# Preparing the second batch and the output weights earlier in a fused attention and FFN layer

## The reference

```python
# B, S, H = 2, 1024, 1024; 32 heads of 32; F = 2752; all float32
x = x + attention(layernorm(x))        # qkv = xn @ Wqkv + bqkv; softmax(q k^T / sqrt(32)) v; ctx @ Wo + bo
xn = layernorm(x)                      # eps 1e-5, no scale or shift
x = x + (silu(xn @ Wg.T) * (xn @ Wu.T)) @ Wd.T
```

## Time and profile before

| | us |
|---|---|
| median of 3 runs | 3329.88 |
| lowest and highest run | 3327.52, 3333.98 |
| profiled execution, its own time | 3327.03 |
| its span in the profile | 3325.2 |
| PE busy | 3191.2 (96%) |
| DVE busy | 2013.0 (61%) |
| ACT busy | 1450.3 (44%) |
| POOL busy | 811.9 (24%) |

### The profile page before, as it was taken

The page is one execution under the profiler, slowest core; times in us unless marked ns, Lnnn a source line. Parts: engine busy times, 40 slices in busy tenths (PEclk is TensorE's granted clock), DMA queues, the critical chain, the costliest instruction groups (busy, mean ns, idle before and its releaser), DMA issues.

```text
span 3325.2 us, 38853 instructions
## 1 busy us (share of the span) xinstructions
PE 3191.2 (96%) x14464; PEld 2490.1 (75%) x14464; DVE 2013.0 (61%) x3093; ACT 1450.3 (44%) x2679; POOL 811.9 (24%) x604
## 2 busy tenths in 40 slices
PE   6999999988999999999799999999999999999999
PEld 5767777766777676776477888888888888888887
DVE  5789888887898888988774433232333423232324
ACT  1477787766777777778552111111111111111111
POOL 1224333332343343433433110101011010101010
PEclk9999999999999999999899999999999999999999
DMA  2434243342333433324556621111111411111111
GB/s 102 124 111 132 84 125 103 102 149 80 102 112 101 124 87 102 120 90 124 152 143 207 207 80 42 60 51 39 57 62 47 171 64 51 39 45 57 51 51 51
DMA packets 146028, 315.90 MB, mean 95 GB/s; under 512 B 24944, under 2 KB 58864, under 8 KB 142256
## 3 DMA queue, kind: packets, MB, share of 16 engines
q1 hardware_dynamic: 145840, 313.42, 30.3%
HBM read 228.41 MB, written 84.41 MB: 94 GB/s over the span
## 4 chain that ended last, share of the span: by engine, by line
PE 84%; DVE 13%; ACT 1%; DMA 1%; issue 1%; SPq 0%; POOL 0%; ACTq 0%; DVEq 0%
PE ps L659 16%; PE ps L660 15%; PE ps L661 15%; PE ps L725 6%; PE ps L744 6%; PE ps L756 5%; PE ps L761 5%; PE ps L814 5%; PE ps L815 5%; PE ps L816 5%; DVE mx L1046 4%; DVE pl L1068 4%; DVE wl L1018 2%; PE ps L686 1%; ACT ph L884 1%
## 5 line engine op out<-in xcount | busy, mean ns | idle before, releaser
L883 ACT ACTIVATE pu<-ps 128x512 f32<-128x512 f32 x1024 | 617.5, 603 | 412.0 <-PE ps L744 409.1
L1046 DVE TENSOR_REDUCE mx<-ps 128x1 f32<-128x512 f32 x1024 | 697.6, 685 | 157.1 <-PE ps L725 147.5
L1146 POOL TENSOR_TENSOR pl<-pu,ph 128x512 fp32r<-128x512 f32 x320 | 434.3, 1357 | 1011.6 <-ACT ph L884 1010.7
L884 ACT ACTIVATE ph<-ps 128x512 fp32r<-128x512 f32 x1024 | 616.4, 602 | 0.0
L1068 DVE TENSOR_TENSOR pl<-pu,ph 128x512 fp32r<-128x512 f32 x704 | 561.7, 798 | 65.1 <-ACT ph L884 62.0
L659 PE MATMUL ps<-x2h,gh 128*128 128x512 f32 x1376 | 535.4, 389 | 0.8 <-DVE x2l L1012 0.8
L660 PE MATMUL ps<-x2h,gl 128*128 128x512 f32 x1376 | 535.3, 389 | 0.0
L661 PE MATMUL ps<-x2l,gh 128*128 128x512 f32 x1376 | 535.3, 389 | 0.0
L1108 DVE TENSOR_TENSOR hf<-ps,sg 128x512 f32<-128x512 f32 (+1 forms) x88 | 60.9, 692 | 694.6 <-PE ps L661 685.9
L725 PE MATMUL ps<-kst,qst 96*128 96x512 f32 x1024 | 422.1, 412 | 38.1 <-DVE mx L1046 37.0
L744 PE MATMUL ps<-qst,kst 98*128 98x512 f32 x1024 | 413.2, 404 | 4.4 <-ACT ph L884 4.1
(11 more groups left out here) (91 smaller groups left out, 4607.7 us busy)
## 6 DMA issues: line engine op xcount, KB each, us to landing
wraw<-in_wqkv SPq DMA_DIRECT2D x24, 1024.0 KB, 5.7
qst<-q_d SPq DMA_DIRECT2D x192, 128.0 KB, 3.0
kst<-k_d SPq DMA_DIRECT2D x192, 128.0 KB, 3.1
graw<-in_wg SPq DMA_DIRECT2D x44, 512.0 KB, 4.6
graw<-in_wu SPq DMA_DIRECT2D x42, 512.0 KB, 3.6
draw<-in_wd SPq DMA_DIRECT2D x42, 512.0 KB, 4.0
q_d<-stg SPq DMA_DIRECT2D x64, 256.0 KB, 2.4
k_d<-stg SPq DMA_DIRECT2D x64, 256.0 KB, 2.3
```

What stands on the lines that cost most here:

```text
L883: e.activation(pu[sl][:, :], bk[:, :], ACT.Exp, scale=SCALE).then_inc(s["a_p"], 1)
L884: e.activation(ph[sl][:, :], bk[:, :], ACT.Exp, scale=SCALE).then_inc(s["a_ph"], 1)
L1046: e.reduce_max(mx[:, j % 2, t, half:half + 1], ps[2 + bank_of["a", j, t, half]][:, :], AX.X).then_inc(s["v_mx"], 1)
L1146: e.tensor_tensor(pl[sl][:, :], pu[sl][:, :], ph[sl][:, :], ALU.subtract).then_inc(s["g_pl"], 1)
```

## The change

1. The kernel's build takes 2 KB for the descriptor scratch in each SBUF partition where it was 16 KB. The zone in which tiles are placed by hand can then be 14 KB longer.
2. `turn[1]` has five places (141, 145 and 149 KB in the zone, which are new, and the two of `stg`). Tiles 0 to 2 are loaded at the last chunk of batch 0's Q and K without a wait, and normalized there. `nready`, a step without instructions, stands for a tile that PE may transpose 4 units after its `nnorm`.
3. Tiles 0 and 1 are transposed between the two last K halves of batch 0, since their 256 columns of `xh` are done with after the first of them. Tile 2 follows right behind the second, and tiles 3 to 7 stay one V tile further ahead than before.
4. Wo's quarters 0 and 1 are loaded during the last Q chunk, and split while PE does the last K half of batch 1 (their columns of `xh` are free then). `oraw`, `ct`, `xr` and the bias have other places; `ct` of tile 0, `xr` of tiles 0 and 1 and the bias are loaded before the projection, and the bias no longer waits for Wo.
5. In the last head (steps 1008 to 1023) all `pl` are on DVE.

The diff, its core (the removed code for output tile 0's late sum is shown by its first lines):

```diff
-    follow["oload"] = lambda i: [(6 + n, ("ohi", i, n)) for n in range(4)]
-    follow["boload"] = lambda: [(8, ("xbo", 0)), (11, ("xbo", 1))]
+    follow["oload"] = lambda i: [(10 + n, ("ohi", i, n)) for n in range(4)] if i > 1 else []
+    follow["olo"] = lambda i, n: [(1, ("oload", i + 2))] if i < 2 and n == 3 else []
+    follow["nnorm"] = lambda n, t: [(4, ("nready", n, t))]
...
         if c == B * KT - 1 and what == 1:
-            step("oload", 0)
+            defer(1, "oload", 0)
+            defer(2, "oload", 1)
+            defer(4, "ctload", 0)
+            defer(6, "boload")
+            for n in range(2):
+                defer(8 + 2 * n, "xrload", n)
+                defer(18 + 2 * n, "xbo", n)
+        if c == KT - 1 and what == 0:
+            for t in range(3):
+                defer(2 + 3 * t, "nload", 1, t)
         for half in range(2):
             if c == KT - 1 and what == 1 and half == 1:
-                until("wlo", NW, 3)
-                defer(1, "nload", 1, 0)
-                defer(1, "nload", 1, 1)
+                yield from turned(0)
+                yield from turned(1)
+                defer(5, "nload", 1, 3)
+            if c == B * KT - 1 and what == 1 and half == 1:
+                for i in range(2):
+                    for n in range(4):
+                        defer(2 + 4 * i + n, "ohi", i, n)
             yield from bank()
...
     def second_batch():
-        defer(7, "nload", 1, 2)
-        defer(8, "nload", 1, 3)
-        yield from turned(0)
-        yield from turned(1)
+        defer(5, "nload", 1, 4)
+        yield from turned(2)
...
-            if t + 2 < TT:
-                yield from turned(t + 2)
+            if t + 3 < TT:
+                yield from turned(t + 3)
...
     def project(b):
         if b == 0:
-            split_o(0, 1)
-            while ("qkst", B * KT - 1, 1, 1) not in made:
-                yield None
-            defer(3, "oload", 1)
...
+            until("qkst", B * KT - 1, 1, 1)
+            defer(2, "ctload", 1)
+            defer(4, "xrload", 2)
+            defer(14, "xbo", 2)
+            defer(16, "ctload", 2)
...
 def on_pool(n):
-    return n % 16 in POOL_PL
+    return n % 16 in POOL_PL and n // 16 < ALL - 1
...
-        turn = {1: [at(f"turn1_{t}", (32, 36, 40, 44)[t if t < 2 else 2 + t % 2], [P, H]) for t in range(TT)],
+        turn = {1: [at(f"turn1_{t}", (145, 149, 141, 40, 44)[t % 5], [P, H]) for t in range(TT)],
...
-        ct = [at(f"ct{i}", 8 * i, [P, 2, KT, P], f32r) for i in range(3)]
-        xr = [at(f"xr{i}", (24, 28, 44)[i], [P, H]) for i in range(3)]
-        oraw = [at(f"oraw{i}", 32 + 8 * i, [P, KT, 256]) for i in range(2)]
-        bo_b = at("bo_b", 40, [P, H])
+        ct = [at(f"ct{i}", (0, 8, 24)[i], [P, 2, KT, P], f32r) for i in range(3)]
+        xr = [at(f"xr{i}", (145, 149, 44)[i], [P, H]) for i in range(3)]
+        oraw = [at(f"oraw{i}", (32, 16)[i], [P, KT, 256]) for i in range(2)]
+        bo_b = at("bo_b", 141, [P, H])
...
-                    pool.wait_ge("p_qk", of_qk(B * KT - 1, 1, 1))
+                    pool.wait_ge("p_qk", of_qk(B * KT - 1, 1, i // 2))
...
-    nc = bacc.Bacc("TRN2", target_bir_lowering=False, num_devices=1)
+    nc = bacc.Bacc("TRN2", target_bir_lowering=False, num_devices=1, dynamic_dma_scratch_size=2048)
```

More of the change, by code:

```diff
@@ L148, in turned @@
     def turned(t):
-        while ("nnorm", 1, t) not in made:
+        while ("nready", 1, t) not in made:
             yield None
@@ L156, in turned @@
             yield 2
+        if t + 5 < TT:
+            defer(2, "nload", 1, t + 5)
     def second_batch():
[L159 to L162 removed]
+        defer(5, "nload", 1, 4)
+        yield from turned(2)
         loaded(NW + 1)
@@ L173, in second_batch @@
         yield from qk_chunk(KT, 1)
-    def split_o(i, units):
-        for n in range(4):
-            defer(units + n, "ohi", i, n)
     def project(b):
         if b == 0:
-            split_o(0, 1)
-            while ("qkst", B * KT - 1, 1, 1) not in made:
-                yield None
-            defer(3, "oload", 1)
[L186 to L195, removed]
+            until("qkst", B * KT - 1, 1, 1)
[3 more added lines that the diff above has]
+            defer(16, "ctload", 2)
         for t in range(TT):
@@ L200, in project @@
                     yield None
-                if n == 0 and half == 1:
-                    defer(3, "boload")
                 yield from bank()
@@ L207, in project @@
                         groups.append(("osum", n, half))
-                        if n:
-                            defer(2, "osum", n, half)
+                        defer(2, "osum", n, half)
                     yield 3
-                if n == 0 and half == 1:
-                    while ("xbo", 0) not in made:
-                        yield None
-                    step("osum", 0, 0)
-                    defer(1, "osum", 0, 1)
-                if n == 0 and half == 0:
-                    continue
-                if half == (n == 0) and n + 2 < B * TT:
+                if half == 0 and 3 <= n + 2 < B * TT:
                     while n + 2 == TT and ("cst", B * KT - 1, 1) not in made:
@@ L529, in on_pool @@
 def on_pool(n):
-    return n % 16 in POOL_PL
+    return n % 16 in POOL_PL and n // 16 < ALL - 1
 def pool_lows(n):
-    return n // 16 * len(POOL_PL) + sum(m < n % 16 for m in POOL_PL)
+    heads = min(n // 16, ALL - 1)
+    return heads * len(POOL_PL) + (sum(m < n % 16 for m in POOL_PL) if heads < ALL - 1 else 0)
 class Line:
@@ L1209, in sp_program @@
                     if n == 1:
-                        if t < 2:
-                            sp.wait_ge("v_wl", of_split(NW))
-                        elif t < 4:
-                            sp.wait_ge(f"d_stg{t % 2}", 32 * (of_qk(KT - 1, 1, 1) // 2))
-                        else:
-                            sp.wait_ge("p_tr", of_tr(1, t - 2, 1))
+                        if t in (3, 4):
+                            sp.wait_ge(f"d_stg{t - 3}", 32 * (of_qk(KT - 1, 1, 1) // 2))
+                        elif t > 4:
+                            sp.wait_ge("p_tr", of_tr(1, t - 5, 1))
                         src = x[1, tile_of(t), :]
@@ L1312, in sp_program @@
                     elif i == 1:
-                        for n in range(2):
-                            sp.wait_ge(f"d_stg{n}", 32 * (of_qk(B * KT - 1, 1, 1) // 2))
+                        sp.wait_ge("p_qk", of_qk(B * KT - 1, 0, 1))
                     else:
@@ L1342, in sp_program @@
                     elif n == 2:
-                        sp.wait_ge("v_ol", 16)
-                    else:
-                        sp.wait_ge("p_qk", of_qk(B * KT - 1, 1, 1))
-                        sp.wait_ge("p_v", of_v(B * NG - 1, TT - 1))
+                        for i in range(2):
+                            sp.wait_ge(f"d_stg{i}", 32 * (of_qk(B * KT - 1, 1, 1) // 2))
+                    else:
+                        sp.wait_ge("p_tr", of_tr(1, TT - 1, 1))
                     copy(xr[n % 3][:, :], x[b, tile_of(t), :], f"d_xr{n % 3}")
```

10 lines of the change are left out of this document (3 added, 7 removed).

## The result

The changed kernel takes 3303.44 us (median of 4 runs, 3301.68 to 3305.58), the kernel before, measured beside it, 3331.93 us (4 runs, 3327.52 to 3334.93). The ratio is 0.9916, interval 0.9899 to 0.9933: 28.5 us faster, where the forecast's sum was 34.6. Of the two profiled executions one took 3301.68 us (span 3300.1), the other 3327.03 (span 3325.2), so the traces have 25.1 us to explain.

The account below looks back on a forecast made before the run. PE, busy 96% of the span, was taken as the bound, with winnable idle time and lower clock in the two handovers. Gains 17.2 + 16.9 + 0.5 = 34.6 us gave 3293 us, range 3275 to 3314.

Parts of the forecast that it names:

- Handover 1: The 82 steps from 663.3 to 822.6 us, with the 18 steps before it: 159.3 us falls to 142.1, gaining 17.2.
- DVE's work at 88.8%: Both handovers: DVE's work is conserved, at plain attention's busy share; 126.2 us gives 142.1, 124.18 gives 139.8.
- "half" rival: Both handovers: PE still waits, for banks, POOL's bunch and the second eight splits; 17.6 us gained, 3309 us; chance 20%.
- no wait for `turn`: Handover 1: a sign that the forecast is right, no wait of PE for `turn` above 1 us.
- Handover 2: The 80 steps from 1545.1 to 1704.8 us: 19.9 us gained by DVE's floor, less 3 for POOL, so 16.9.
- POOL's bunch: Handover 2: two bias sums and three splits close together on POOL make a `pl` late, costing 3 us, between 0 and 5.
- The clock: Both handovers: granted clock over 0.95 if the forecast is right; below 0.9 it is wrong.
- the rival that ended slower: Both handovers: frequent short PE pauses lower the clock; slower from a granted clock of some 0.78, 3346 us at 40%; chance 6%.
- Last head: End of the attention stage: five `pl` go from POOL to DVE, gaining 0.5 us, between -1 and 1.5.
- scratch, 0: Descriptor scratch: no compute instruction touches it and no transfer queue shown needs it, so 0 us.
- DVE denser: Both handovers: DVE fills its gaps and PE's floor decides; up to 64.6 us gained, 3262 us, midway 3278; chance 10%.
- Nothing: Both handovers: starved steps are caught up anyway, only the order changes; 3327 to 3330 us; chance 4%.

Follow-up runs that it names:

- `v_weights_later`: The changed kernel with batch 1's first V weights loaded, and so split, after the transposes of tiles 0 and 1: 3300.49 us (one run).
- `bias_moved`: The changed kernel with bias and residual loads earlier, two bias sums ahead of Wo's splits and the third behind them: 3299.97 us (one run).
- `halves_first`: The changed kernel with output tiles 0 to 2 done left halves first, Wo's last eight splits spread, loads and third bias sum moved: 3293.88 us, ratio 0.9890.
- `best_again`: Repeat run of `halves_first` plus the first two bias sums ahead of Wo's splits and batch 1's V weights after the first transposes: 3290.37 us, ratio 0.9899.
- `last_head_pool`: The changed kernel with the last head's five `pl` given back to POOL: 3304.52 us (4 runs), ratio 0.9923.
- `scratch_only`: The kernel before with the 2 KB descriptor scratch and nothing else: 3331.01 us (10 runs), ratio 1.0003.

## Why the prediction was right, and where not

**Right in kind, and inside the range.** The changed kernel is faster, 3303.44 us for 3293 forecast, inside 3275 to 3314. It is 28.5 us faster in one comparison and 22.0 in the other, where the sum said 34.6. The reading that only the two handovers can give anything held: nothing outside them moved by more than 1.9 us, and identical code between steps 434 and 904 moved by 2.8 us among the runs of this study (720.7 to 723.5).

**Handover 1, 17.2 forecast, 15.1 measured.** The sum, DVE's work at 88.8%, came close, in part by luck: two errors of opposite sign. DVE's work was 123.4 us (28.56 + 10.99 + 83.83) where 126.2 was taken, and DVE was 85.6% busy and not 88.8%; the stage took 144.2 us where 142.1 was forecast, and 146.4 in the mean of the seven traces. The work is 2.8 us smaller mostly by the norms (9.5 us for eight before, 5.3 for the six now in the stretch). What replaced the wait for `turn` is what the "half" rival named, transposes that wait for banks, with 10.1 us instead of 12.4; but its cost in the span was the 2.1 us short (5.7 in the longest of the seven) and not 8.6. The predicted "no wait for `turn`" holds. `v_weights_later` shows that the place of the V splits is not what holds the stage.

**Handover 2, 16.9 forecast, 9.7 measured: the mis-sized term.** The step that failed is "DVE's work is 124.18 us, at 88.8% 139.8", less 3 us for POOL's bunch. Two things were wrong with it. First, DVE's work was not conserved: 128.69 us, and the whole growth is one row, the 16 `xl` from 14.7 to 19.8 us, because bias sums of POOL now run beside them; before, the first of them (1649.6 us) came 18 us after the last split of Wo (1631.0). At 88.8% those 4.5 us are 5.1 us of time. The prediction saw this contention, and let it count for the rival alone. `bias_moved` and the splits' own durations beside a bias sum show the contention; that run also shows that it isn't got rid of by moving the sums, which then stretch `pl`. Second, the density: DVE was 85.8% busy over the handover, which is another 5.1 us (128.69 us of work at 85.8% and at 88.8%). Two batches of eight splits with too little between them make DVE and PE late in turns, at mean clocks of 0.67 and 0.81. The 3 us for POOL's bunch were not seen where they were put: 5.1 + 5.1 - 3 are the 7.2 us missing. Their mechanism, a late `pl` on POOL, no wait of PE shows. `halves_first` reaches 139.6 us with 125.8 us of DVE work, that is 90.1%: the forecast's 139.8 can be reached, but not with this order. Nor is 88.8% of DVE a floor; the prediction called it one, though it added that DVE can be denser. `best_again` did the handover in 136.6 us with 125.67 us of DVE work, 92.0%. By the pair of `halves_first` and the changed kernel, the second batch as it stood cost 10.4 us (150.0 - 139.6).

The page "SBUF — State Buffer" of the Trainium skill, section "Who interferes with whom", has the rule for the first of these: a DVE instruction with two SBUF inputs contends with a GpSimd instruction that reads SBUF. This trace agrees and gives it a size: `xl` from SBUF took up to 2834 ns beside a bias sum, and 682 ns at the median once the roundings were on ACT. The prediction's other half, that a DVE instruction with a single SBUF input does not contend, leaves out the condition of that page of the Trainium skill, "outside the 2-port perf modes", and does not hold for this kernel: a norm (L1003, one SBUF tile in) takes 804 ns alone, and of the eight of the earlier trace rows the four that run for 0.89 us or more beside a POOL `pl` or `ca` take 1437 to 1684.

**The clock.** Forecast over 0.95 in both handovers. Handover 1 has 0.99 in the changed kernel's trace and 0.94 to 0.97 in the six others with the same program, so it holds in most of them only. The row of `bias_moved`, for all 82 steps:

```profile
663.70:811.50 147.80, 132.47 (x651) 97.70 (x650) 123.72 (x199) 105.19 (x204) 45.69 (x38) 0.94 0.37 111
```

Handover 2 does not have it (0.91). It was above the 0.9 below which the forecast would have counted as wrong, and far from the 0.78 of the rival that ended slower. That rival's result is excluded. Its mechanism is not: with 12 short waits of up to 2.7 us in the rows above, the clock of handover 1 came out between 0.94 and 0.99.

**The other signs.** No wait for `xr` is left, as forecast, but PE still waited for Wo's low parts, 5.7 us where none was forecast. ACT's last exponential starts 24.8 us earlier, for 34. DVE's work grew by 4.5 us in handover 2 and fell by 2.8 in handover 1, under the 5 us that would have counted as wrong.

**Last head, 0.5, and scratch, 0.** Both are 0 as measured; the 0.5 us isn't shown by `last_head_pool` (1560.4 against 1561.0 behind step 1023), and lies within what that stretch varies in the other traces with it (1560.2 to 1561.7).

**The other rivals.** "DVE denser" needed more than 88.8% busy; the changed kernel had 85.6 and 85.8%. "Nothing" is excluded by the interval. "Half" had the right mechanism at handover 1 (waits for banks), and at handover 2, for its eight splits but not for POOL's bunch, and nearly the right size there: 8.5 for 9.7. The result lies between it and the forecast, and the traces' 25.1 us are a little nearer to its 17.6 than to 34.6.

**Left open.** Why the eight steps of the first batch of splits still take 21.4 us with both sums moved (25.6 without), was not settled, nor which part of `halves_first` brought its gain, nor what keeps handover 1 at 144 to 148 us. Nor was the changed kernel tried with DVE's `xl` on another engine.

## What to carry to other kernels

Where an engine is the second bottleneck, take its busy time in a stage over the density that it reaches next door as an estimate of that stage, and not as a floor. It gave 142.1 us for 144.2 to 147.8, and 139.8 for 150.0, which became 139.6 and then 136.6 once the work was laid out otherwise. Such work is conserved only if its neighbours on the other engines are: list which SBUF-to-SBUF instructions of DVE will now run beside POOL's, and price them by their stretched duration and not by the mean. Moving the neighbour may only move the stretching to another instruction. And splits that are needed in a batch are worth laying apart, with other work for PE between them: here the same 108 matmuls went from 38.1 to 26.6 us.

## What the runs showed that was not expected

The same instructions in the same stretch can run at different clocks from one execution to the next. Steps 370 to 378 have the same program in the changed kernel and in `bias_moved`; the first took 13.9 us at 1.00 (shown above), the second:

```profile
695.00:710.80 15.80, 15.27 (x56) 10.61 (x55) 11.11 (x18) 10.90 (x22) 2.58 (x2) 0.78 0.36 116
```

Steps 410 to 434 in the old order took, in the kernel before,

```profile
769.40:822.60 53.20, 42.02 (x222) 31.61 (x222) 39.21 (x61) 30.85 (x62) 12.51 (x10) 0.94 0.23 70
```

and in `scratch_only`, with the same program there:

```profile
769.90:827.40 57.50, 47.19 (x222) 35.88 (x222) 39.27 (x61) 30.81 (x63) 12.69 (x10) 0.82 0.23 65
```

In the new order they take 38.7 us in every one of the ten traces that have it, at 1.00. What decides between the levels was not tried. That PE pauses less in the new order there (busy 37.2 of 38.7 us, before 42.0 of 53.2), and that the clock is then the same each time, fits the reading that pauses put the clock of what follows at hazard, by 4 us here; it isn't shown. It doesn't carry over to the whole handover, which varies by 3.6 us in the new order and by 4.4 in the old.
